# An output projection taken apart into fp16 products and spread over attention and feed-forward

## The reference

```python
x = x + attn(layernorm(x), w_q, w_k, w_v, w_o)   # x: 2 x 1024 x 512, 32 heads of 16
x = x + ffn(layernorm(x), w_gate, w_up, w_down)  # inner width 1376
# attn: softmax(q k^T / 4) v, heads joined, then einsum('bse,oe->bso', out, w_o)
# ffn: int4_quant(x) -> gate, up with ternary weights; int8_quant(up * relu(gate)^2) -> ternary w_down
```

## Time and profile before

| what | value |
|---|---|
| median of 3 runs | 969.07 us (967.86 to 973.85) |
| profiled execution | 970.29 us, span of its instructions 968.5 us |
| mean granted clock of PE | 0.979 of 2.4 GHz |
| busy share of the span | PE 95%, DVE 88%, ACT 80%, POOL 14% |
| attention units | about 83 us to 779 us |
| feed-forward stages | from 779 us to the end |

### The profile page before, as it was taken

One profiled execution on the slowest core, in us unless ns is written; L12 is line 12 of the kernel. 1 busy time (PEld: TensorE's weight loads), 2 busy tenths in 40 slices (PEclk: granted clock), 3 DMA queues, 4 the chain that ended last, 5 costly groups with the idle time before them and its releaser, 6 DMA issues.

```text
span 968.5 us, 16815 instructions
## 1 busy us (share of the span) xinstructions
PE 919.0 (95%) x5934; PEld 300.9 (31%) x5934; DVE 851.1 (88%) x1513; ACT 772.3 (80%) x1437; POOL 140.1 (14%) x286
## 2 busy tenths in 40 slices
PE   4898999999999999999999999999898999999985
PEld 3333222222222222222222222222112245555542
DVE  7898899999999999999999999999877177877773
ACT  5653498999899998899998999898785877777773
POOL 3411011121111211112111121110002011112100
PEclk9999999999999999999999999999788999999997
DMA  9720021021121113102112111316540033111000
GB/s 353 228 90 1 0 71 41 24 56 51 50 56 40 40 35 80 41 23 57 54 47 55 40 42 37 78 40 178 185 104 12 12 130 111 45 44 55 22 24 32
DMA packets 38010, 64.92 MB, mean 67 GB/s; under 512 B 3622, under 2 KB 18982, under 8 KB 37670
## 3 DMA queue, kind: packets, MB, share of 16 engines
q1 hardware_dynamic: 37926, 63.85, 22.3%
HBM read 42.27 MB, written 21.23 MB: 66 GB/s over the span
## 4 chain that ended last, share of the span: by engine, by line
PE 80%; DVE 5%; ACT 4%; issue 2%; DMA 1%; SPq 1%; POOL 0%; ACTq 0%; POOLq 0%; DVEq 0%
PE ps L410 25%; PE ps L390 14%; PE ps L354 13%; PE ps L332 8%; PE ps L580 6%; PE ps L549 6%; PE ps L605 3%; DVE mx L1007 3%; PE ps L296 2%; DMA qk<-att_d 1%; ACT PB L744 1%; PE ps L371 1%; PE ps L595 1%; DVE hm L1103 1%; ACT XV L804 1%
## 5 line engine op out<-in xcount | busy, mean ns | idle before, releaser
L1007 DVE TENSOR_REDUCE mx<-ps 128x1 f32<-128x512 f32 x1024 | 632.5, 683 | 24.5 <-PE ps L354 18.1
L744 ACT ACTIVATE PB<-ps 128x512 f32<-128x512 f32 x1024 | 542.7, 597 | 77.0 <-PE ps L390 76.3
L354 PE MATMUL ps<-QK 48*128 48x512 f16 x1024 | 306.1, 388 | 9.3 <-DVE mx L1007 5.3
L390 PE MATMUL ps<-QK 50*128 50x512 f16 x1024 | 297.1, 388 | 3.5 <-ACT PB L744 2.5
L410 PE MATMUL ps<-PB,Vg 128*32 128x512 f32 x2048 | 278.1, 616 | 0.2 <-ACT PB L744 0.2
L390 PEld LDWEIGHTS ps<-QK 50*128 50x128 f16 x1024 | 70.9, 94 | 205.1 <-ACT PB L744 166.6
L354 PEld LDWEIGHTS ps<-QK 48*128 48x128 f16 x1024 | 76.0, 94 | 181.7 <-DVE mx L1007 152.2
L332 PE MATMUL ps<-XV,wqk 128*128 128x512 f16 x384 | 102.5, 385 | 0.0
L1282 POOL TENSOR_SCALAR nmb<-nm 128x16 f16<-128x16 f32 x32 | 6.5, 203 | 543.5 <-DVE nm L1012 543.5
L549 PE MATMUL ps<-wo,XV 128*128 128x512 f32 x128 | 63.1, 621 | 3.0 <-POOL XV L1327 3.0
L410 PEld LDWEIGHTS ps<-PB,Vg 128*32 128x32 f32 x2048 | 40.6, 108 | 69.6 <-ACT PB L744 36.8
(11 more groups left out here) (133 smaller groups left out, 652.6 us busy)
## 6 DMA issues: line engine op xcount, KB each, us to landing
parts_d<-spl SPq DMA_DIRECT2D x64, 128.0 KB
att_d<-OS SPq DMA_DIRECT2D x32, 256.0 KB
QK<-parts_d SPq DMA_DIRECT2D x48, 128.0 KB, 3.9
QK<-parts_d SPq DMA_DIRECT2D x16, 256.0 KB, 4.5
XV<-att_d SPq DMA_DIRECT2D x2, 2048.0 KB, 12.0
wqk<-x SPq DMA_DIRECT2D x16, 256.0 KB, 3.6
QK<-rden_d SPq DMA_DIRECT2D x8, 512.0 KB, 7.9
out<-PB SPq DMA_DIRECT2D x16, 256.0 KB, 2.0
```

The source lines that it names most:

```text
L354: nc.tensor.matmul(ps[:, at % S_BANKS, :], QK[rows, sup % 2, 2 * set_ + p, 0, half * HALF + qt * P:half * HALF + (qt + 1) * P], QK[rows, s ...
L390: nc.tensor.matmul(ps[:, T_BANK + n % T_BANKS, :], QK[rows, sup % 2, 2 * set_ + p, 1, kt * P:(kt + 1) * P], QK[rows, sup % 2, 2 * set_ + p ...
L744: nc.scalar.activation(PB[:, at % 3, i, :], ps[:, T_BANK + n % T_BANKS, :], ACT.Exp, scale=exp_reg).then_inc(probs, 1)
L1007: nc.vector.tensor_reduce(mx[:, v % 2, idx, kh:kh + 1], ps[:, at % S_BANKS, :], AX.X, ALU.max).then_inc(s_used, 1)
```

## The change

The output projection uses fp16 halves of `wo` and of the quotient, with the same three products as the jobs: 12 fp16 matmuls for a tile in place of four fp32 ones. Splitting `wo` takes the norm of its entries (a pass on ACT in unit 20, a small matmul and five small DVE operations in unit 21), a scaled copy on ACT in unit 22 and a remainder on DVE in unit 23. POOL has three operations for a tile (`pool_att`) in place of one. Tiles 0 to 3 take the place of the job in units 26 to 29; ACT copies them out of PSUM and POOL adds the residual. Tiles 4 to 7 lie in the ramp, three matmuls in a step. Tiles 8 to 15 are one run of 96 matmuls, of which stages 3 to 11 take ten each and stage 12 six. The reciprocal of batch 0 moves to unit 19. Of the four sums of absolutes two stay in units 28 and 29 and two go into the ramp; the twelve DVE passes over the down weights come behind the first two tiles' quantisation. The value weights' scale is undone by a constant.

```diff
-MEAN_BANK = (3, 3, 2)
+MEAN_BANK = (3, 3, 1)
+FIRST_OUT = 26
+UNIT_TILES = 4
+OUT_FROM, OUT_PIECES = 3, 10
...
         def pe_ramp_step(pe, sup, step):
-            if step == RAMP:
-                pe.wait_ge(s_used, SUP_ITEMS * SUPERS)
-                pe_mean(pe, 2)
-            pe_attention_out(pe, (step - RAMP) // 4, step % 4)
             pe_scoresT(pe, sup, step, 0)
...
+            if step == RAMP:
+                pe.wait_ge(s_used, SUP_ITEMS * SUPERS)
+            if step == RAMP + 6:
+                pe_mean(pe, 2)
+            n = step - RAMP
+            for m in range(3):
+                pe_attention_out(pe, UNIT_TILES + n // 4, n % 4 * 3 + m)
...
         def o_bank(t):
-            return (0, 2, 0, 1)[t] if t < O_AHEAD else 0
+            return av_bank(FIRST_OUT + t + 1) if t < UNIT_TILES else (0, 2, 0, 1)[t - UNIT_TILES] if t < BT else 0
-        def pe_attention_out(pe, t, g):
-            if g == 0:
+        def pe_attention_out(pe, t, m):
+            k, (a, b) = m // 3, PRODUCTS[m % 3]
+            if m == 0:
                 pe.wait_ge(att_ready, t + 1)
...
-                    pe.wait_ge(x2_ready, t - 1 if t <= O_AHEAD else t)
-            last = nc.tensor.matmul(ps[:, o_bank(t), :], att[:, t % 2, g, :], wo[:, g, :],
-                                    start=(g == 0), stop=(g == SPB - 1))
+                elif t >= UNIT_TILES + 2:
+                    pe.wait_ge(x2_ready, t - UNIT_TILES - (1 if t <= BT else 0))
+            last = nc.tensor.matmul(ps[:, o_bank(t), :], att[:, t % 2, a, k * P:(k + 1) * P], wop[:, b, k, :],
+                                    start=(m == 0), stop=(m == 3 * KT - 1))
...
         def pe_tile(pe, t):
-            if t + O_AHEAD < TILES:
-                for g in range(SPB):
-                    pe_attention_out(pe, t + O_AHEAD, g)
+            if t >= OUT_FROM:
+                for n in range((t - OUT_FROM) * OUT_PIECES, min((t - OUT_FROM + 1) * OUT_PIECES, BT * 3 * KT)):
+                    pe_attention_out(pe, BT + n // (3 * KT), n % (3 * KT))
...
+        def act_out_copy(act, t):
+            act.wait_ge(o_psum, t + 1)
...
+            nc.scalar.activation(qk32[:, t % 2, :], ps[:, o_bank(t), :], ACT.Copy, scale=oscale[:, 1:2]).then_inc(o_copy, 1)
...
+                if (at, r) == (20, 4):
+                    act_squares(act, 3)
+                if (at, r) == (22, 4):
+                    act_weights(act, 3, 0, HID)
-                if last and step in (4, 6, 8, 10):
-                    act_abs(act, 2, (step - 4) // 2)
+                if last and step in (2, 10, 17, 20):
+                    act_abs_down(act, (2, 10, 17, 20).index(step))
...
-                if n == (SUPERS - 1) * SUP_ITEMS + AHEAD + 7:
+                if n == 19 * UNIT_ITEMS + AHEAD + 16:
                     dve_reciprocal(dve, 0)
+                elif n == 21 * UNIT_ITEMS + AHEAD + 9:
+                    dve_total_squares(dve, 3)
+                elif n == 21 * UNIT_ITEMS + AHEAD + 22:
+                    dve_scales(dve, 3)
+                    dve_out_scale(dve)
+                elif n == 23 * UNIT_ITEMS + AHEAD + 4:
+                    dve_weights(dve, 3, 0, HID, 6)
...
         def dve_tile(dve, t):
-            if t + O_AHEAD < TILES:
-                dve_x2(dve, t + O_AHEAD)
+            for n in range(BT):
+                if t == OUT_FROM + (n * 3 * KT + 3 * KT - 1) // OUT_PIECES:
+                    dve_x2(dve, BT + n)
...
         def pool_att(pool, t):
-            nc.gpsimd.tensor_tensor(att[:, t % 2, :, :], num[b][:, :, at:at + P], rdn[:, b, :, at:at + P], ALU.mult)\
-                .then_inc(att_ready, 1)
+            nc.gpsimd.tensor_tensor(w.rearrange("p (g t) -> p g t", g=SPB), num[b][:, :, at:at + P], rdn[b][:, :, at:at + P], ALU.mult)\
+                .then_inc(att_step, 1)
+            cast(att[:, t % 2, 0, :], w).then_inc(att_step, 1)
+            nc.gpsimd.tensor_tensor(att[:, t % 2, 1, :], w, att[:, t % 2, 0, :], ALU.subtract).then_inc(att_ready, 1)
```

More of the change, by code:

```diff
@@ L368, in pe_max_rows @@
                 pe.wait_ge(os_copy, unit - 1)
+            if unit == 22:
+                pe.wait_ge(wn_tot, 4)
             dst = ps[0:2 * GH, av_bank(unit + (1 if unit == 0 else 0)), :].bitcast(FP16)
@@ L570, in pe_gate_up @@
                     pe.wait_ge(x2_ready, 2)
-                    for w in range(3):
+                    for w in range(2):
                         pe.wait_ge(w_tern[w], 4)
+                    pe.wait_ge(probs, 4 * UNITS * KEYT - 2)
                 else:
@@ L602, in pe_down @@
                 pe.wait_ge(o_ready, t)
+            else:
+                pe.wait_ge(w_tern[2], 4)
             for k in range(IT):
@@ L719, in act_abs, with act_abs_down @@
         def act_abs(act, w, q):
-            if wsum_first(w, q):
-                act.wait_ge(raw_in[w // 2], 16 * (4 + w // 2))
-                if w == 2:
-                    act.wait_ge(down_zero, 1)
+            if wsum_first(w, q) and w == 0:
+                act.wait_ge(gate_in, 16 * 4)
             nc.scalar.activation(ternq(w, q), raw(w, q), ACT.Abs, accum_out=wsum[:, w, q:q + 1]).then_inc(w_abs[w], 1)
+        def act_abs_down(act, q):
+            act.wait_ge(down_in[q // 2], (32, 48)[q // 2])
+            if q == 0:
+                for r in range(2):
+                    act.wait_ge(parts_out[r], 32 * 2 * SUPERS)
+            else:
+                act.wait_ge(w_abs[2], q)
+            if q == 2:
+                act.wait_ge(down_zero, 1)
+            nc.scalar.activation(spl[:, :, :, :].rearrange("p s a n -> p (s a n)").bitcast(BF16)[:, 0:DQ], raw(2, q), ACT.Abs,
+                                 accum_out=wsum[:, 2, q:q + 1]).then_inc(w_abs[2], 1)
+        def act_out_copy(act, t):
+            act.wait_ge(o_psum, t + 1)
+            if t == 0:
+                act.wait_ge(os_ready, 1)
+                act.wait_ge(job_split, JOBS)
+            elif t >= 2:
+                act.wait_ge(x2_pool, t - 1)
+            nc.scalar.activation(qk32[:, t % 2, :], ps[:, o_bank(t), :], ACT.Copy, scale=oscale[:, 1:2]).then_inc(o_copy, 1)
         def act_sign(act, w, q, order):
@@ L1148, in dve_early_tiles @@
                     dve_quant(dve, 0)
+            dve_x2(dve, UNIT_TILES)
+            dve_total(dve, 2)
+            dve_factor(dve, 2)
+            for q in range(4):
+                dve_round(dve, 2, q, q)
+                if q == 3:
+                    dve.wait_ge(att_ready, BT)
+                dve_ternary(dve, 2, q, q)
+            nc.vector.tensor_scalar(wfd[:], wfac[:, 2:3], 1.0 / 127.0, None, ALU.mult)
             dve_xq_copy(dve, 0)
-            dve_x2(dve, 2)
-            dve_x2(dve, 3)
+            for t in range(UNIT_TILES + 1, BT):
+                dve_x2(dve, t)
         def dve_tile(dve, t):
@@ L1395, in _ @@
                     pool_rstd(pool, t + 2)
-                if t + O_AHEAD < TILES:
-                    pool_att(pool, t + O_AHEAD)
+                for n in range(BT):
+                    if t == (2, 3, 4, 5, 6, 7, 8, 10)[n]:
+                        pool_att(pool, BT + n)
         xt = x.rearrange("(t p) n -> p t n", p=P)
```

266 lines of the change are left out of this document (157 added, 109 removed).

## The result

The changed kernel takes 998.16 us (median of 4 runs, 995.06 to 998.77) where the kernel before takes 968.47 us (4 runs, 965.51 to 973.85): a ratio of 1.0294, 95% interval 1.0259 to 1.0329, so it is slower by 3%. One run each of `e8_all` (1229.61 us, granted clock 0.66) and of the kernel before (2910.14 us) was disturbed and stands in no median or ratio here. The profiled execution took 997.91 us, its span 996.1 us, which is 27.6 us more than the span before.

What follows compares the result with a forecast made beforehand. DVE was taken to bound attention, PE the stages with projection, ACT and DVE the others. Terms -0.3, +11.0, -6.9, -9.4, -5.9, +18.8, +13.8 sum to +21.1 on 970.3: 991.4, or 990 us against the median, range 966 to 1003.

Steps and rivals of the forecast that it cites:

- The wait in the middle of a stage: Stages 4 to 7, 10, 11: the next tile's first matmul waits for dve_x2; +18.8 us, plus +13.8 for the clock.
- rival (d): POOL's three operations for a tile get into DVE's way in eight stages: +11 us, 1001 us; chance 11%.
- Rival (b): The mid-stage wait is hidden and the change does what fewer PE cycles promise: 952 us; chance 9%.
- (a): The mid-stage wait is there, but the clock stays up: 976 us; chance 12%.
- (c): Wait as forecast at full clock, ACT's passes free, excess of units 28 and 29 all gone: 967 us; chance 8%.
- The clock: Half clock behind each of six mid-stage waits, 2.3 us each: +13.8 us, between 0 and +17.
- the 996 us: Alternative total if each mid-stage wait loses half of the whole 6.6 us throttled time, 3.3 us.
- Units 19 to 23: Attention: reciprocal, norm and wo remainder on DVE 6.4 us, two ACT passes 4.6 us; +11.0, between +6.4 and +16.
- Units 26 to 29: Late attention units lose the reciprocal (2.3 us) and two sums of absolutes (4.6 us): -6.9, between -11.6 and -4.
- The ramp: Ramp: sixteen shorter steps -3.5 us and 5.9 us won at the start: -9.4, between -12 and -6.
- Stages without a wait: Stages 0 to 2, 3, 8, 9 at 10.39 us in place of 11.37: -5.9, between -6 and -4.
- The start: Front of the kernel: DVE loses two operations on single columns; -0.3 us, between -1 and 0.

Runs made afterwards that it cites:

- e8_all: Changed kernel with twelve matmuls in each of eight stages, wo remainder and ACT passes in four pieces, batch 1 reciprocal halved, norm matmul earlier: 952.54 us, ratio 0.9838.
- e3_fill: Changed kernel with 14 to 20 extra matmuls ahead of each waiting matmul, keeping PE busy through the wait: 981.36 us, ratio 1.0152 to the kernel before.
- e1_twelve: Changed kernel with twelve projection matmuls in each of stages 3 to 10, so every tile ends with its stage: 956.60 us, ratio 0.9895 to the kernel before.
- e4_before_mid: Kernel before, all fp32, with its projection shifted by half a tile so that tiles end in the middle of stages 1 to 11: 1027.08 us (one run).
- e9_before_sums: Kernel before with its four ACT sums of absolutes at steps 4, 7, 10, 13 in place of 4, 6, 8, 10: 967.16 us (one run).
- e7_recip: e1_twelve with the reciprocal of batch 1 in two halves, the first in DVE's idle time ahead of stage 0's quantisation: 955.20 us (one run).

## Why the prediction was right

The forecast was 990 us in a range of 966 to 1003, slower with a chance of 0.72; it is 998.16 us. The sign and the main mechanism were right, and the sum was 8.2 us low: 6.5 us in its terms (+27.6 us in the spans, +21.1 forecast), and the rest, but for rounding, because the profiled execution of before lay 1.2 us above its median, that of after 0.3 us below.

**The wait in the middle of a stage.** It stands where the prediction put it, in the stages it named, with idle times of 3.67 to 5.02 us, 28.3 us in all. Forecast +32.6, measured +33.3; its two halves were less exact than their sum, and that their errors cancel is luck. The wait at full clock is 21.3 us by `e3_fill` where the forecast had 18.8, and the clock is 12.0 us where it had 13.8. Of the 2.5 us that are missing in the first half, 1.6 are POOL, the mechanism of rival (d). A DVE operation of 0.23 us (L1130), which stands three places ahead of `dve_x2`, took up to 1.16 us where it meets POOL's operations:

```profile
863.33 1.16 DVE L1130 TENSOR_SCALAR agu<-wgu,bsum 128x3 f32<-128x3 f32 x1
864.99 0.75 DVE L1091 SCALAR_TENSOR_TENSOR wqk<-ps,oscale,wqk 128x512 f32<-128x512 f32 x1
```

In the six stages `dve_x2` began 3.23 us after the start of the maximum before the change, and now 3.33, 3.72, 4.16, 3.24, 3.30 and 3.23: 1.6 us in sum, not the 11 us of the rival. The other 1.0 us are some 0.17 in every stage: `dve_x2` takes 0.74 us and not 0.68, and the handover to PE about 0.15 us and not 0.06. In stages 2 and 3, which have no wait, POOL costs nothing (10.40 us, with three of its operations between the maxima of 2 and 3); in stage 8 `dve_x2` is 0.45 us late and the stage lasts 10.62 us. Rival (b), the hidden wait, is out by `e1_twelve` and `e4_before_mid` from both sides; rivals (a) and (c), which want the clock to stay up, by the windows above.

**The clock.** `e3_fill` prices it at 1.6 to 2.6 us in the six stages (each stage with the clock down against the same stage with the clock up), `e4_before_mid` at 1.69 us. The forecast of 2.3 us came from the 6.6 us of the earlier trace rows. The form in which the prediction had it, half of the lower stretch that falls behind the restart, fits all six. In stages 5, 6 and 7 the lower level lasted 3.4 us, all of it behind the restart, and they lost 1.67, 1.63 and 1.67 us. In stages 4, 10 and 11 it lasted 6.8 us and began while PE still stood; 4.3, 5.4 and 4.6 us of it lay behind the restart at 830.77, 918.48 and 936.27, and they lost 2.12, 2.64 and 2.28 us. Here is almost the whole of it in stage 4:

```profile
828.30:835.00 6.70, 4.01 (x10) 1.51 (x12) 3.87 (x12) 2.15 (x2) 1.80 (x3) 0.50 0.00 0
```

It began 2.3 to 5.2 us after the idle time did; the "1 to 4 us" of the prediction should have been 3 to 4 by its own.

The Trainium skill, TensorE: Matmul & The Clock Gate, section HAM oscillation, counts the loss as half of the throttled time. In stages 5 to 7 that is 1.7 us each, and this trace agrees. In stages 4, 10 and 11 it would be 3.4 us each, more than the 2.1 to 2.6 us that they lost, because 1.5 to 2.5 us of the throttled time passed while PE stood anyway. So by this measurement only what lies behind the restart counts. That the 996 us which the prediction set beside its sum by that rule are nearer to 998.16 is luck: 3.3 us for a wait are 19.8 us, and the clock cost 12.0.

**Units 19 to 23.** Forecast +11.0, measured +12.1. The reciprocal cost 1.47 us (forecast 1.75), the norm 1.9 (2.3), the two ACT passes 1.8 and 1.9 (2.3 each), all a little less. The step that failed is the remainder, taken at the 2.34 us of its twin: its unit grew by 5.05 us. DVE took 2.93 us, its first 0.8 us beside POOL's subtraction, and the clock fell behind the idle time. Of the 5.05 us, 2.6 are there in every kernel that was run and up to 2.4 more in five of the seven with the one long operation.

**Units 26 to 29.** Forecast -6.9, measured -9.0, because each sum of absolutes that stayed costs 1.0 us and not the 2.3 us that the prediction took from the crowded units of before. The mean clock over units 28 and 29 is 1.00 now, and by `e9_before_sums` half clock behind the crowded sums is the rest of that price.

**The ramp.** Forecast -9.4, measured -8.5. The twelve passes began 19 us into it, and the copy of the transposed tile 0 was done before tile 7's matmul wanted it, as forecast.

**Stages without a wait.** Forecast -5.9, measured -3.9. The step that failed is "10.39 in place of 11.37" for stage 0, which takes 12.10 us, more than the 10.97 of before. The reciprocal of batch 1, an operation of 1.72 us, stands in it ahead of the inner products. Before, its projection kept PE at work; without it PE stands 2.54 us and the clock is at half for the three microseconds from 791 us on:

```profile
788.25 0.79 PE L621 MATMUL ps<-identb,spl 128*128 128x128 bf16 x11 [2.54 <-DVE spl L1187]
```

```profile
791.00:794.00 3.00, 2.81 (x10) 1.50 (x11) 1.86 (x5) 1.49 (x4) 0.00 (x0) 0.50 0.35 134
```

The growth is that half clock. Here are the gate products that wait for DVE behind the reciprocal, in the kernel before and in the changed one:

```profile
792.96 0.76 PE L580 MATMUL ps<-tu,Vg 128*128 128x344 bf16 x4 [1.56 <-DVE XV L1092]
```

```profile
791.19 1.33 PE L606 MATMUL ps<-tu,Vg 128*128 128x344 bf16 x4 [1.57 <-DVE XV L1161]
```

Both start 7.94 us after the start of stage 0's maximum (785.02 and 783.25 us). From there to the next maximum (795.99 and 795.35 us) it is 3.03 us before and 4.16 us after, which is the 1.13 us that the stage grew by; four of the products take 1.33 us where they took 0.76. The other 0.58 us above 10.39 are there at full clock too; the forecast had nothing for the reciprocal in this stage. `e7_recip` took 0.75 us out of it by moving half of the reciprocal; a run with the clock kept up there was not made.

**The start.** Forecast -0.3, measured +3.7, and this is no effect of the change. In the kernels here the first last reduction lies between 82.03 and 85.15 us, and the second interval behind it between 19.97 and 23.59 us, with no order that follows an edit. To the third last reduction the kernels with the attention part of before take 133.4 to 135.2 us, those with that of the changed kernel 132.3 to 137.1. The second interval follows the granted clock in it. The busy time over this interval in the changed kernel, then in `e1_twelve`:

```profile
113.53:137.12 23.59, 23.20 (x128) 5.12 (x128) 19.96 (x33) 17.55 (x34) 1.39 (x5) 0.78 0.16 34
```

```profile
113.89:133.86 19.97, 19.15 (x128) 4.93 (x128) 19.82 (x33) 17.46 (x34) 1.39 (x5) 1.00 0.19 41
```

In the kernel before the clock was 0.92 there, and the interval 21.39 us. Why it differs between runs of the same instructions, no run here shows. The two traces that were compared happened to differ by 3.7 us up to there, 2.2 of it in this interval; with the forecast's -0.3 this is 4.0 of the 6.5 us that the terms were low.

## What to carry to other kernels

A tile of accumulation should end where the stage ends, as long as the next one starts in the same bank (two banks in turn were not tried here). The matmul that starts the new tile waits for the read-out, and everything behind it in PE's list waits too, so ask at which place in the reader's order the read-out stands. The cheaper instructions saved 0.9 us in a stage, and their placement cost 6. Where one long operation is put between short ones that feed another engine, try it in pieces: the two ACT passes in four pieces each gave 2.6 us back, and the DVE remainder in four pieces took away a loss of 1.2 to 2.4 us that five of seven kernels showed, so a single run without the loss is no proof that there is none.
